# Second attention's gate weight and rank blocks staged in the output weight's tile; the output weight loaded last

## Time and profile before

| | |
|---|---|
| median of three runs | 3125.68 us |
| lowest and highest | 3124.5 and 3126.15 us |
| span of the profiled execution | 3127.1 us |
| TensorE busy (matmul) | 3004.2 us, 96% of the span |
| VectorE busy | 2367.4 us, 76% |
| ScalarE, GpSimd busy | 744.8 us, 1044.8 us |
| DMA | 153.91 MB in all, mean 49 GB/s |

### The profile page before, as it was taken

The page is one execution under the profiler, slowest core; times in us unless marked ns, Lnnn a source line. Parts: engine busy times, 40 slices in busy tenths (PEclk is TensorE's granted clock), DMA queues, the critical chain, the costliest instruction groups (busy, mean ns, idle before and its releaser), DMA issues.

```text
span 3127.1 us, 126889 instructions
## 1 busy us (share of the span) xinstructions
PE 3004.2 (96%) x54866; PEld 2270.9 (73%) x54932; DVE 2367.4 (76%) x5409; ACT 744.8 (24%) x1357; POOL 1044.8 (33%) x1398
## 2 busy tenths in 40 slices
PE   3699999999999999999999999999999999999995
PEld 2577777777777777777777777777777777777663
DVE  6867777777777777777777777777777777777775
ACT  2222222222222222222222122222222222222211
POOL 2023333333333333333333333333333333333333
PEclk9799999999999999999999999999999999999997
DMA  5212222222232222322222222222222222222210
GB/s 173 67 39 49 44 45 51 42 50 46 42 51 44 46 48 46 50 42 47 49 42 48 48 46 45 48 45 45 51 43 49 47 42 51 44 46 48 46 40 24
DMA packets 384396, 153.91 MB, mean 49 GB/s; under 512 B 352800, under 2 KB 361632, under 8 KB 383904
## 3 DMA queue, kind: packets, MB, share of 16 engines
q1 hardware_dynamic: 383904, 146.02, 24.8%
HBM read 45.29 MB, written 16.78 MB: 20 GB/s over the span
## 4 chain that ended last, share of the span: by engine, by line
PE 93%; DVE 4%; issue 1%; DMA 1%; ACT 0%; POOL 0%; SPq 0%; DVEq 0%; POOLq 0%; ACTq 0%
PE bank L752 22%; PE bank L753 21%; PE bank L754 21%; PE bank L1038 8%; PE bank L917 3%; PE bank L832 3%; PE bank L870 3%; PE bank L990 2%; PE bank L710 2%; PE bank L847 2%; PE bank L889 2%; PE bank L1013 2%; PE bank L1000 1%; DVE absmax L1177 1%; PE bank L1026 1%
## 5 line engine op out<-in xcount | busy, mean ns | idle before, releaser
L672 POOL TENSOR_TENSOR work<-work 128x512 f32<-128x512 f32 x128 | 185.6, 1450 | 659.2 <-DVE work L1433 659.2
L752 PE MATMUL bank<-xaT,wq_hi 128*128 128x128 f16 x2048 | 359.9, 220 | 6.3 <-DVE wk_lo L1202 4.0
L753 PE MATMUL bank<-xaT,wq_hi 128*128 128x128 f16 x2048 | 359.9, 220 | 0.0
L754 PE MATMUL bank<-xaT,wq_lo 128*128 128x128 f16 x2048 | 359.9, 220 | 0.0
L752 PE MATMUL bank<-xaT,wk_hi 128*128 128x128 f16 x2048 | 358.8, 220 | 0.0
L753 PE MATMUL bank<-xaT,wk_hi 128*128 128x128 f16 x2048 | 358.6, 220 | 0.0
L754 PE MATMUL bank<-xaT,wk_lo 128*128 128x128 f16 x2048 | 358.5, 220 | 0.0
L752 PE MATMUL bank<-xbT,wb 128*128 128x128 f16 x2048 | 348.3, 220 | 0.0
L753 PE MATMUL bank<-xbT,wb 128*128 128x128 f16 x2048 | 347.6, 219 | 0.6 <-issue 0.6
L754 PE MATMUL bank<-xbT,wb 128*128 128x128 f16 x2048 | 347.5, 219 | 0.0
L1322 DVE TENSOR_SCALAR work<-bank,eps_q 128x256 f32<-128x256 f32 x256 | 123.0, 481 | 178.7 <-PE bank L754 178.7
(11 more groups left out here) (210 smaller groups left out, 8243.0 us busy)
## 6 DMA issues: line engine op xcount, KB each, us to landing
xin<-in_L_attn_a_x SPq DMA_DIRECT2D x64, 256.0 KB, 2.6
out<-xf SPq DMA_DIRECT2D x64, 256.0 KB, 2.1
table<-in_tables SPq DMA_DIRECT2D x64, 192.5 KB, 2.6
work<-in_L_attn_a_Wq SPq DMA_DIRECT2D x1, 2048.0 KB, 7.9
work<-in_L_attn_a_Wk SPq DMA_DIRECT2D x1, 2048.0 KB, 12.9
wb<-in_L_attn_a_Wv SPq DMA_DIRECT2D x1, 2048.0 KB, 17.6
work<-in_L_attn_a_Wo SPq DMA_DIRECT2D x1, 2048.0 KB, 8.4
work<-work SPq DMA_TRANSPOSE x128, 3.9
```

What stands on the lines that cost most here:

```text
L672: pool.tensor_tensor(to[:, :, :, :], to[:, :, :, :], cross[:, :, ::-1, :], ALU.add)\
L752: nc.tensor.matmul(o, a[0], b[0], start=first, stop=False)
L753: nc.tensor.matmul(o, a[0], b[1], start=False, stop=False)
L754: return nc.tensor.matmul(o, a[1], b[0], start=False, stop=last)
```

## The change

The three staging places `g`, `rk` and `rq` move from `work` to the first 2048 columns of `wout`, which are the whole of that tile (8 KB a partition). Their three loads move from slot 2 to where the load of `wout` stood, behind `xTa_t` of chunk 0, and wait for nothing. The load of `wout` moves to slot 3, behind the place of `nf1_rs` in the list, where VectorE does `lo rq`; it waits on SP until `rq` has been read. The position of every other step is as it was; so are VectorE's, ScalarE's and TensorE's instruction streams, but for the place from which `g`, `rk` and `rq` are read.

```diff
@@ LATE
-    (2, "qk0_e"): ("lo bk", "load g", "load rk", "load rq"),
+    (2, "qk0_e"): ("lo bk",),
@@
-    (3, "nf1_rs"): ("lo rq",),
+    (3, "nf1_rs"): ("lo rq", "load wout"),
@@ wide
+        staged = wout[:, :, :].rearrange("p k n -> p (k n)")
@@
-                "g": work[:, 8192:9216],
-                "rk": work[:, 9216:9728], "rq": work[:, 9728:10240], "bv": work[:, 6144:8192], "out": work[:, 6144:8192]}
+                "g": staged[:, 0:1024], "rk": staged[:, 1024:1536], "rq": staged[:, 1536:2048], "bv": work[:, 6144:8192], "out": work[:, 6144:8192]}
@@ SP
+            def load_wout():
+                taken(sp, "rq")
+                sp.dma_start(wout[:, :, :], out_w.rearrange("(k p) n -> p k n", p=P)).then_inc(s_wout, 16)
+
@@
             xTa_t(first_chunk(sp, "xTa_t"))
-            sp.dma_start(wout[:, :, :], out_w.rearrange("(k p) n -> p k n", p=P)).then_inc(s_wout, 16)
+            for n, src in (("g", g_w), ("rk", ranks[1]), ("rq", ranks[0])):
+                load(n, src)
@@
-                 "load g": lambda: load("g", g_w, "bk"), "load bv": lambda: load("bv", v_w, "bq"),
-                 "load rk": lambda: load("rk", ranks[1], "bk"), "load rq": lambda: load("rq", ranks[0], "bk")})
+                 "load bv": lambda: load("bv", v_w, "bq"), "load wout": load_wout})
```

## The result

The changed kernel takes 3133.64 us (median of ten runs, 3131.75 to 3134.92), the kernel before beside it 3127.0 us (ten runs, 3124.5 to 3128.62). The ratio is 1.0022, 95% interval 1.0012 to 1.0031: **slower by 0.22%**, +6.6 us. The prediction was 3130.0 us, +4.3 us on 3125.68, with a range from 3125.8 to 3132.8. So 1.3 of the missing 3.6 us is the base, which three runs had put too low, and 2.3 are cost. Run again, the changed kernel gave 1.0017 (1.0008 to 1.0026), +5.0 us. The side and the place were right, the size was not.

The account below looks back on a forecast made before the run. TensorE, busy for 96% of the span, was taken as the bound except in set-up, where the change acts. The terms 0 + 0 + 3.9 + 0.4 = +4.3 us on 3125.7 gave 3130.0 us, range 3125.8 to 3132.8.

Parts of the forecast that it names:

- Part 1: Slot 2: the loads of g, rk and rq leave SP's queue, all off the chain; worth 0.
- Part 2: SP's start: three loads where wout's stood, same bytes, some 1 us more of SP; worth 0.
- `bq` would land 0.3 us later at most: Slot 2: two transpositions directly behind bq delay it by 0.3 us, hidden in 0.52 us to spare; taken as 0.
- The slow rival: Slot 2: transpositions moved beside bq land it 2.6 us later, costing 2.1; sum 6.4, 3132.1 us; chance 0.15.
- its sign: Idle time of VectorE before the maximum of bq, released by a DMA; would show the forecast wrong.
- Part 3: Slot 3: wout, waiting for lo rq, holds xTa_t of chunk 2; TensorE starts at 148.5 instead of 144.68, +3.9 us.
- the row of slot 2: Three loads of 1 MB at 107.05, a transposition behind them landing 6.41 us after the first load's issue.
- The estimate by the fit of the Trainium skill: Slot 3: wout occupies the queue for 2.4 us, xTa_t lands at about 147.5; +2.9 instead of +3.9.
- The rival in which the megabyte doesn't hold the transposition: Slot 3: only SP's wait counts, +0.9 us and about +0.2 for the clock, 3126.8 us; chance 0.12.
- Part 4: Slot 3: TensorE restarts at half clock, losing 2.1 us against 1.7 before; +0.4 us, between 0.2 and 1.
- The forecast's own case: Whole kernel: slower by +2.4 to +5.8 us, at 3130.0 us; chance 0.70.
- up to 1.9 us that idle time of TensorE might swallow: Between 145 and 260 us: unexplained idle time of TensorE could absorb up to 1.9 us; taken as 0.

Follow-up runs that it names:

- the run with both alone: The change with wout's load moved further back in slot 3, behind both transpositions of the attention's output: 3125.94 against 3126.84 us for the kernel before (0.9998).
- Part 3 alone: The kernel before with only wout loaded late, in slot 3 behind the wait for rq and ahead of xTa_t: 3132.09 against 3126.84 us (1.0018).
- the megabyte alone: The kernel before with wout loaded directly ahead of xTa_t of chunk 2, without any wait for rq: ratio 0.9997.
- inputs first: The kernel before with slot 1's loads of rhs and bk put behind ld_x of chunk 1 on SP: 3120.24 against 3125.91 us (0.9984).
- both: The kernel before with rhs and bk loaded behind ld_x of chunk 1, and bv staged early in wout's tile: 3119.27 against 3125.91 us (0.9979).

## Why the prediction was right and wrong

**Part 1 and Part 2, 0: right as far as the time can tell**, by the run with both alone (0.9998). The loads of `g`, `rk` and `rq` were hidden, and taking away hidden transfers gave nothing. One judgement inside failed: `bq` would land 0.3 us later at most, by the row of `rhs`. It lands 1.0 us later. The row was of two plain loads one behind the other; transpositions behind a load delay it more, so that the 0.52 us of slack were used up and 0.4 to 0.5 us of idle time appeared. The slow rival named this mechanism with 2.6 us, 2.1 of them as cost; it exists at 1.0, with 0.4 to 0.5 as cost. So its sign appeared, VectorE's idle time with a DMA as releaser, but not its price.

**Part 3, +3.9: right**, in mechanism and nearly in size. By its own terms it is 3.8 (148.5 less 144.68). The transposition landed 6.6 us after `wout`'s issue, 6.4 were taken from the row of slot 2; the offset grew by 4.2 us in all three profiles that have both halves of it, and by 0.7 or 0 in those with one. One row beside it was misread: `k_w` landed 2.7 us after `rhs`, not 2.3, as it was also issued 0.4 us later; that changes nothing in the argument. The estimate by the fit of the Trainium skill ("DMA: Bandwidth & Descriptors", anatomy of one DMA), +2.9 (2.8 by its terms), is at least 1.3 too low here. It is given for another path, and `wout` itself took 5.6 us to land where it gives 4.4; the measurement decides. The rival in which the megabyte doesn't hold the transposition falls by 6.1 against 3.0 us.

**Part 4, +0.4: the step that failed.** It charged the changed kernel for a slow restart and took off the 1.7 us that the clock cost the kernel before in its one profile, as if it always did. It doesn't: its third profile, and six of the seven variants whose `qk0` has VectorE as its releaser, lost nothing there. The changed kernel lost it in both of its profiles, as Part 3 alone did. By the mark "to load" the term lies between 0.2 us (19.58 against 19.38) and 2.0 (19.76 against 17.76) from execution to execution, not between 0.2 and 1. With Part 3's 4.2 us that makes 4.4 to 6.2, and with the 0.4 to 0.5 of `bq` 4.8 to 6.7. If the clock falls in three of ten executions without the late load, as in the ten profiles above, the term is 1.4 us on average and the changed kernel's sum about 6.0; that is an estimate from few profiles. The three measured costs are 5.0, 5.25 (without `bq`'s part) and 6.6, the last with an interval of 3.8 to 9.7, so the term's size is shown by the profiles and not by the times.

**The base.** The first three executions of the kernel before had a median 1.3 us below that of ten, which no step of the reasoning could see. It counts: on its own base the prediction's range is +0.1 to +7.1 us, and +6.6 lies in it; 3133.64 us is above 3132.8 only with the base's 1.3 us. The forecast's own case, +2.4 to +5.8, holds +5.0 and not +6.6. Its lower half stood on up to 1.9 us that idle time of TensorE might swallow. None was swallowed: the changed kernel is 7.5 us later at SP's load of chunk 3 (171.58 against 164.06), 7.5 at that of chunk 4 and 7.9 at that of the last chunk.

**What stays open: 7.5 us in the profiles.** In this pair of profiles 2.8 us are made up only behind the last chunk's load, where the three profiles of the kernel before alone differ by 5 us (170.8 to 175.9). Of the 7.5 us offset and clock make 4.4; the other 3.1 are there when `lo rq` starts. Part 3 can't reach back there, and of Part 1 only `bq`'s 0.5 us is seen. SP's rows for the two profiles show where they arise: 0.75 us up to SP's load of `Wo` (`Wq` landed after 8.7 us, not 7.9), 1.15 from there to that of `rhs`, 0.5 from there to that of `bv`, the size of `bq`'s idle time, and 0.75 from there to `lo rq` (`bv` landed after 5.6 us, not 5.0). In the second stretch the change has moved nothing, and TensorE's clock was lower. The windows from 48 to 64 us of the kernel before and of the changed kernel (columns as in the earlier trace rows):

```profile
48.00:64.00 16.00, 12.26 (x177) 8.71 (x177) 9.13 (x15) 4.77 (x3) 0.00 (x0) 0.89 0.01 2
```

```profile
48.00:64.00 16.00, 11.61 (x166) 8.83 (x167) 7.99 (x15) 4.77 (x3) 0.00 (x0) 0.79 0.01 2
```

The mean is 0.89 in all three profiles of the kernel before and 0.79 in the three with the late load ahead of `xTa_t`, but also 0.79 with the megabyte alone, with inputs first and with both, of which none has a loss in time. Where it is 0.79 the stretch from `Wo` to `rhs` takes 30.3 to 30.4 us, elsewhere 29.3 to 29.6. So this much of the 3.1 us belongs to the execution that the profile took; that the three with the loss all drew it is taken for chance, which three profiles can't prove.

## What to carry to other kernels

An early load that nobody waits for is no gain; before moving a load, look for the one whose landing an engine waits for. What does cost is the place of a load in its queue: a load with a wait holds every issue behind it, and its bytes then hold them a second time, so add the two before comparing with the slack of the first input behind it. Put waiting weight loads behind the inputs of the next step, not ahead; here that one edit was worth 5.7 us where the change lost 5.0 to 6.6.

## What the runs showed of the hardware

- Two transpositions by DMA issued directly behind a 1 MB load (`bq`) make it land 0.4 to 1.2 us later (5.7 to 6.1 against 4.9 to 5.3 us); `rhs`, with 1 MB of plain load directly behind, lands after 5.3 to 5.6. `xTa_t` with a megabyte of plain load ahead lands after 6.0 to 6.2 us, alone after 3.0 to 3.1. The order in the queue holds the later one back, but does not fully shield the earlier.
- After the same 2.02 us of idle time in the same kernel TensorE's granted clock fell to half (1.2 GHz) in two profiles and stayed at full (2.4 GHz) in a third; over ten profiles of eight kernels it fell in three. After 6.2 us of idle time it was at half in three of three. One profile of the clock is one draw.
